# Making the second LayerNorm, the row table and the router's logits inside the attention units of a one-core transformer block

## What is computed

```python
mod = (silu(c) @ wmod).reshape(8, 6, 1, -1)          # sa, ca, ga, sb, cb, gb for each batch
ga, gb = sign(ga) * max(|ga|, 0.25), the same for gb
h = layernorm(x) * (1 + ca) + sa
x = x + ga * attention(h)                            # 16 heads of 16, rope, causal, Wo and bias
h = layernorm(x) * (1 + cb) + sb                     # the second LayerNorm
logits = h @ switch_w + switch_b                     # router over 8 experts, top 1
y = gelu(h @ w1[e] + b1[e]) @ w2[e] + b2[e]          # e = argmax of a token's logits, F = 1024
x = x + gb * (y * max softmax(logits))
```

## Time and profile before

| | before |
|---|---|
| median of 3 runs | 946.27 us |
| the three runs | 940.78, 946.27, 946.91 us |
| the profiled execution's own time | 946.43 us |
| its span, first to last instruction | 944.7 us |
| PE, DVE, ACT, POOL busy | 82%, 70%, 51%, 32% of the span |
| PE's mean granted clock | 0.899 of full |

### The profile page before, as it was taken

One profiled execution on the slowest core, in us unless ns is written; L12 is line 12 of the kernel. 1 busy time (PEld: TensorE's weight loads), 2 busy tenths in 40 slices (PEclk: granted clock), 3 DMA queues, 4 the chain that ended last, 5 costly groups with the idle time before them and its releaser, 6 DMA issues. The chain is left out here.

```text
span 944.7 us, 20373 instructions
## 1 busy us (share of the span) xinstructions
PE 771.2 (82%) x7362; PEld 469.0 (50%) x7362; DVE 659.4 (70%) x1270; ACT 481.4 (51%) x886; POOL 298.7 (32%) x377
## 2 busy tenths in 40 slices
PE   5859999999999999999887737730189999999994
PEld 3423444444444444444433327730177777777773
DVE  4857888788887888878764158879436666666664
ACT  1426666666666666666666115468144444444442
POOL 4303333232232323323222024357303333333331
PEclk9969999999999999999998656555579999999998
DMA  6153000010200102001010067767202222222200
GB/s 203 35 132 81 24 2 1 21 48 1 68 1 17 53 1 68 2 11 35 2 46 1 22 204 244 229 172 230 83 12 82 88 85 84 61 72 78 81 23 1
DMA packets 48523, 63.88 MB, mean 68 GB/s; under 512 B 9028, under 2 KB 42925, under 8 KB 48304
## 3 DMA queue, kind: packets, MB, share of 16 engines
q1 hardware_dynamic: 43440, 45.80, 16.1%
q0 software_dynamic: 4992, 16.81, 5.9%
HBM read 52.71 MB, written 17.73 MB: 75 GB/s over the span
## 5 line engine op out<-in xcount | busy, mean ns | idle before, releaser
L792 DVE TENSOR_REDUCE row_max<-ps_max 128x2 f32<-128x1024 f32 (+2 forms) x192 | 200.0, 1042 | 58.5 <-PE ps_max L461 55.8
L653 ACT ACTIVATE prob<-ps_sc 128x1024 f32<-128x1024 f32 (+1 forms) x192 | 169.3, 882 | 116.0 <-PE ps_sc L488 113.5
L314 POOL TENSOR_SCALAR_AFFINE_SELECT prob<-prob 128x512 f32<-128x512 f32 x128 | 84.0, 656 | 308.6 <-ACT prob L653 308.4
L1428 PE MATMUL ps_h<-tok_t,w_hi 128*128 128x128 f16 x1248 | 140.3, 222 | 2.5 <-issue 1.7
L1428 PEld LDWEIGHTS ps_h<-tok_t,w_hi 128*128 x1248 | 109.9, 99 | 44.2 <-issue 5.7
L1428 PE MATMUL ps_h<-tok_t,w_lo 128*128 128x128 f16 x624 | 122.8, 222 | 0.0
L1444 PE MATMUL ps_y<-w_both,hid_hi 128*128 x312 | 119.6, 384 | 0.8 <-DVE hid_lo L1503 0.8
L1482 ACT ACTIVATE hid<-ps_h,b_t 128x128 f32<-128x128 f32 x312 | 89.0, 372 | 45.3 <-PE ps_h L1428 45.2
L1501 DVE CAST hid_hi<-hid 128x512 f16<-128x512 f32 x78 | 36.7, 470 | 99.4 <-ACT hid L1482 99.3
L501 PE MATMUL ps_pv<-prob,v_sb 128*32 128x512 f32 (+3 forms) x1024 | 97.0, 452 | 0.0
L102 POOL DMA_INDIRECT slots<-row_dram,token x39 | 42.5, 1090 | 165.0 <-DVE y L1517 151.2
(11 more groups left out here) (224 smaller groups left out, 1417.0 us busy)
## 6 DMA issues: line engine op xcount, KB each, us to landing
raw<-w SPq DMA_DIRECT2D x32, 512.0 KB, 5.1
xs<-x SPq DMA_DIRECT2D x8, 512.0 KB, 4.6
xr<-x SPq DMA_DIRECT2D x8, 512.0 KB, 3.6
row_dram<-gates_dram SPq DMA_DIRECT2D x1, 4096.0 KB
row_dram<-xr SPq DMA_DIRECT2D x8, 512.0 KB, 3.5
x<-row_dram SPq DMA_DIRECT2D x8, 512.0 KB, 5.0
row_dram<-rows SPq DMA_DIRECT2D x8, 512.0 KB, 4.4
prob<-wmod SPq DMA_DIRECT2D x1, 1536.0 KB, 8.5
```

Source lines behind the costliest of these rows:

```text
L314: nc.gpsimd.affine_select(out=diag, in_=diag, compare_op=ALU.is_ge, fill=0.0, base=0, pattern=[[0, HG], [1, P]], channel_multiplier=-1).th ...
L653: nc.scalar.activation(p_kb[:, :, first * L:(first + n) * L], ps_sc[:, :, 0:n * L], ACT.Exp, scale=SCALE).then_inc(exp_done, 1)
L792: nc.vector.tensor_reduce(dst, ps_max[:, :, 0:n * L].rearrange("p j (m l) -> p j m l", m=n), AX.X, ALU.max).then_inc(max_done, 1)
L1428: last = mm(o, w[:, :, k, f, :][:, bass.ds(e, 1), :].rearrange("p e m -> p (e m)"), tok_t[:, j % 2, part, k, :], start=(n == 0 and f % HF ...
```

## The change

The work of the second LayerNorm, of the h rows and of the logits leaves `route_part` and goes into the units and the tail of `attention_part`.

- **Rows.** `xr` becomes `rows`, with h in columns 0 to 255 and x1 in 256 to 511, float32, stored as one piece for a batch. After `residual`, DVE does `row_statistics` in shot 2. POOL does `modulate_row` at the end of the unit: a power, one subtract and multiply, one multiply by a row of 1+cb and one add of a row of sb, all 128x256 float32. The rows of ga, 1+cb and sb come by `load_mods`, two batches held at a time. PE no longer makes the transposed form of these modulations.
- **Logits.** Seven units (`LAG`) behind, PE transposes h in shot 0 (`h_transposes`, two float32 transposes), ACT copies (`keep_h`), and once for each batch PE makes eight products and one transpose, with ACT copies.
- **Tail.** Each of the last batch's four tiles has a bank of its own (`tail_banks`). The rows, transposes and logits of the last tiles follow there.
- **`route_part`** holds only routing, b1, b2 and the weight halves: 6 buffers in place of 4, the first four chunks loaded during the last units, no loops. POOL makes the low halves of chunks 0 to 17, DVE those of 18 to 31, after the routing chain. SP stores the probabilities after the load of chunk 24, which waits for DVE's low half of chunk 18. POOL fetches after its 18 chunks.
- **`expert_part`.** The table holds h as float32, so PE makes two float32 transposes for four float16 ones, ACT copies the high half (128x256) and DVE makes the low half (`low_tokens`, 128x256), ahead of `halves(j)`.

```diff
+LAG = 7
+N_RAW = 6
+N_EARLY = 4
+POOL_CHUNKS = 18
...
             for b in range(2, B):
...
+                store_rows(b - 2)
+                load_mods(b)
                 load_xr(b)
+            for n in range(N_EARLY):
+                load_chunk(sp, n)
...
+            def modulate_row(Y):
+                pool.wait_ge(row_var, Y + 1)
+                nc.gpsimd.tensor_tensor(row_rstd[:, at:at + 1], row_eps[:, at:at + 1], neg_half[:, :], ALU.pow).then_inc(row_rs, 1)
...
+                nc.gpsimd.tensor_scalar(h, rows[:, par, t, D:2 * D], row_mv[:, at, 0:1], row_rstd[:, at:at + 1],
+                                        ALU.subtract, ALU.mult).then_inc(row_hat, 1)
+                nc.gpsimd.tensor_tensor(h, h, mod_rows[:, par, 1, :], ALU.mult).then_inc(scaled_done, 1)
+                nc.gpsimd.tensor_tensor(h, h, mod_rows[:, par, 2, :], ALU.add).then_inc(h_done, 1)
...
                 clear_future(U, 3)
+                if U >= QT + 1:
+                    modulate_row(U - QT - 1)
+            for Y in range(NT - QT - 1, NT):
+                modulate_row(Y)
...
+                    if s == 0 and Z >= 0:
+                        pe.wait_ge(gated_done, X)
+                        h_transposes(Z, ps_nd)
+                    if s == 1 and Z >= 0:
+                        pe.wait_ge(htr_kept, Z + 1)
+                        if Z % QT == QT - 1:
+                            logit_products(Z // QT, ps_nd)
+                        if Z % QT == 0 and Z:
+                            logit_transposes(Z // QT - 1, ps_nd)
...
             for X in range(NT - QT, NT):
-                att_transposes(X, NU)
-                project_out(X)
+                att_transposes(X, tail_banks[X % QT])
...
+                project_out(X, tail_banks[X % QT])
...
+            def row_statistics(Y):
+                dve.wait_ge(x1_done, Y + 1)
+                nc.vector.bn_stats(row_bn[:, :], rows[:, par, t, D:2 * D]).then_inc(row_stats, 1)
+                dve.wait_ge(row_stats, Y + 1)
+                nc.vector.bn_aggr(row_mv[:, at, :], row_bn[:, :]).then_inc(row_mv_done, 1)
+                dve.wait_ge(row_mv_done, Y + 1)
+                nc.vector.tensor_scalar(row_eps[:, at:at + 1], row_mv[:, at, 1:2], LN_EPS, None, ALU.add).then_inc(row_var, 1)
...
                     if s == 2 and T + 1 < NT:
                         statistics(T + 1)
+                    if s == 2 and X > 0:
+                        row_statistics(X - 1)
...
+            for n in range(N_RAW, CHUNKS):
+                sp.wait_ge(lo_of[n % N_RAW], turn(n) - 1)
+                load_chunk(sp, n)
+                if n == POOL_CHUNKS + N_RAW:
+                    sp.wait_ge(gate_done, 1)
+                    sp.dma_start(row_dram[:, AT_P:AT_P + 1].rearrange("(t p) o -> p (t o)", p=P), gate_p,
...
+            for n in range(POOL_CHUNKS):
+                pool.wait_ge(scaled_of[n % N_RAW], scaled_turn(n))
+                nc.gpsimd.tensor_tensor(half_of(w1_lo, w2_lo, n), raw_of(n), half_of(w1_hi, w2_hi, n),
+                                        ALU.subtract).then_inc(lo_of[n % N_RAW], 1)
...
-            batches(dve, step)
...
+            for n in range(POOL_CHUNKS, CHUNKS):
+                low_half(n)
...
+            low_tokens(0)
             for j in range(NJ):
+                if j + 1 < NJ:
+                    low_tokens(j + 1)
                 halves(j)
```

More of the change, by code:

```diff
@@ L380, in raw_gates @@
             def raw_gates(ps):
-                for n, part in enumerate((2, 5)):
+                for n, part in enumerate((5, 2)):
                     for k in range(KC):
@@ L386, in raw_gates, with raw_mods @@
                 last.then_inc(gates_ps, 1)
+            def raw_mods(ps):
+                for n, part in enumerate((4, 3)):
+                    for k in range(KC):
+                        last = mm(ps[0:B, n * D:(n + 1) * D], c_t[:, k, :], wmod_sb[:, k, part * D:(part + 1) * D],
+                                  start=(n == 0 and k == 0), stop=(k == KC - 1), skip_group_check=True)
+                last.then_inc(mods_ps, 1)
             pe.wait_ge(silu_done, 1)
@@ L1183, in _, with high_half @@
-            batches(act, step)
+            def high_half(n):
+                at = n % N_RAW
+                act.wait_ge(raw_loaded[at], 16 * turn(n))
+                nc.scalar.activation(half_of(w1_hi, w2_hi, n), raw_of(n), ACT.Copy, scale=W_SCALE).then_inc(hi_of[at], 1)
+                if n < POOL_CHUNKS:
+                    act.wait_ge(hi_of[at], turn(n))
+                    nc.scalar.activation(raw_of(n), raw_of(n), ACT.Copy, scale=W_SCALE).then_inc(scaled_of[at], 1)
+            high_half(0)
@@ L1192, in _ @@
+            for n in range(1, CHUNKS):
+                high_half(n)
         @block.vector
         def _(dve):
[L1194 to L1205 removed]
@@ L1221, in step @@
-            def step(i, u):
-                b = 2 * i + u
-                dve.wait_ge(rs, b + 1)
-                for t in range(QT):
-                    nc.vector.tensor_scalar(xhat[:, t, :], x1[:, u, t, :], mean_var[:, t, 0:1], rstd[:, t:t + 1],
-                                            ALU.subtract, ALU.mult).then_inc(xh, 1)
-                if not (last(i) and u):
-                    statistics(b + 1, 1 - u, 16 * (i + (u + 1) // 2 + 1))
-                if not isinstance(b, int) or b:
-                    e, half = before(i, u)
-                    low_half(e, 2 * half)
-                    low_rows(b - 1, 1 - u)
-                dve.wait_ge(xt_ps, b + 1)
-                for k in range(KC):
-                    nc.vector.tensor_scalar(h_t[:, u, k, :], ps_xt[k][:, :],
-                                            mod_t[:, 4 * KC + k, bass.ds(b, 1)], mod_t[:, 3 * KC + k, bass.ds(b, 1)],
-                                            ALU.mult, ALU.add).then_inc(ht_done, 1)
@@ L1410, in transposes @@
                 pe.wait_ge(slot_loaded[j % NB], loads_before(j))
-                ge(pe, x_kept, j)
-                for n in range(2 * KC):
-                    last = nc.tensor.transpose(ps_x[:, :].bitcast(F16)[:, n * P:(n + 1) * P],
-                                               slots[:, j % NB, 0:D].bitcast(F16)[:, n * P:(n + 1) * P], ident16[:, :])
+                ge(pe, x_lo_done, j)
+                for k in range(KC):
+                    last = nc.tensor.transpose(ps_x[:, k * P:(k + 1) * P], slots[:, j % NB, k * P:(k + 1) * P], ident[:, :])
                 last.then_inc(x_ps, 1)
```

552 lines of the change are left out of this document (256 added, 296 removed).

## The result

The changed kernel takes 915.4 us (median of 4 runs, 912.6 to 916.2) against 944.5 us for the kernel before (4 runs beside it, 940.8 to 946.9): ratio 0.970, with a 95% interval of 0.967 to 0.973. The profiled execution has a span of 913.6 us for 944.7 before, 31.1 us less. 925.3 was forecast for it. So the sign and the range held, and the forecast was 11.7 us too cautious. The working has to be read term by term, because its misses have both signs and partly cancel: that the total came this close is in part luck.

A forecast was written before the change was run, and what follows sets the result against it. PE and DVE in turn were taken to bound the units, and a serial chain and weight loads the gap. 944.7 + 27 + 2.4 - 52.8 + 4 = 925.3 us of span, 927 us time; range 908 to 946.

The forecast's parts named there:

- What bounds the units: Attention units: path runs over DVE in shots 1 to 4, over PE from shot 5 to the next shot 1.
- costs its full length: Units: work added on either engine's own stretch adds fully; statistics 0.81 us, h transposes 0.28 us; all units +27 us.
- my case: Whole kernel: the forecast's main outcome, 927 us, own range 916 to 938 us, chance 0.50.
- the first rival: Units pay 10 us, not 27, PE being about as late as DVE in shots 2 and 3; 910 us, chance 0.20.
- The tail: Last copy of u to route part: separate banks save, added rows and logits cost; 26.4 us for 24.0, +2.4.
- The chain: Routing chain: 25.9 us without POOL's hold-ups, plus 19 operations lengthened by 1.8 us, 60 us; bounds 48 and 65.
- Behind the chain: Chain's end to PE's first expert work: b2 operations, low halves, chunk turns, SP transfers 20 us, plus 1.7 to PE's start.
- The gap as a sum: Route part to PE's expert start: 0.3 + 60 + 20 + 1.7 = 82 us for 134.8, -52.8.
- the gap is set by the weights, not the chain: Gap rival: 32 chunks at 3.1 us each take 99 us, +17 on 82; 944 us, chance 0.06.
- The experts: Expert tiles: two float32 transposes cost PE more than four float16 ones, +2.3 to 5.5 us, taken as +4.
- the slower outcome: Units: PE's clock falls as its busy share drops to some 90%; +46 us, 973 us, chance 0.08.
- POOL's row operations blocked nothing on DVE in the units: Units, rival judged here: POOL's row operations block DVE about 0.6 us a unit, +17 us; 944 us, chance 0.16.

The follow-up runs named there:

- two edits: Changed kernel with row statistics moved to shot 0, ratio 0.968; changed kernel with the probabilities' store behind chunk 12 and b2 transfers behind all chunks, ratio 0.969.
- a third: Changed kernel with six slot buffers and the last four rows' 128x256 operations on DVE, held against six buffers alone (0.957): ratio 0.954.

## Why the prediction was right, and where it was not

Forecast minus measured, the spans differ by 11.7 us: units 8.5 too dear, tail 0.7 too cheap, gap 5.4 too cheap, experts 9.2 too dear. The sum came out near because two misses went against the other two.

**What bounds the units** was read rightly. Work put on DVE between shot 1 and the maxima of shot 3 showed as PE's wait of 0.70 us. Work put on PE in shot 0 cost 0.22. But "costs its full length" was too much: 1.09 us a unit was forecast and 0.68 measured. The statistics cost 0.56 and not 0.81. They moved the maxima by 0.73, and PE gave 0.12 of its wait back in shot 5, where it had stood a little for ACT's exponentials: its scores there began 0.23 us behind the max scores' last products before, and 0.11 after. That makes 0.78 us in three units of four. In the fourth this wait for the exponentials was longer,

```profile
298.77 0.29 PE L488 MATMUL ps_sc<-q_t,k_t 64*128 64x128 f16 x4 [0.33 <-ACT prob L653]
```

and such a unit took 15.09 us and not 14.70. The longer unit absorbs this whole, so the fourth unit costs only 0.39 more, and the mean is 0.68. I had added the two costs to a mean that held these idle times. The logit products, 1 us in the forecast, cost nothing: all units from the eighth on take 15.48. The lead (up to the seventh copy) and the last units cost 2.5 and 2.4 us, for 1.6 and 3.0 in the forecast. Of the 2.5, 1.4 lie ahead of the first copy of u, which comes anywhere from 85.7 to 88.0 us in executions of kernels that are alike up to there. The sum is +18.5 and not +27, within the bounds of 10 and 40 and halfway between my case and the first rival's 10. That rival's reason was that PE is about as late as DVE in shots 2 and 3. In the kernel before it was so, to within 0.1 us (PE's products ahead of shot 4 start at 310.27 and take 1.07), but this saved only 0.03 of the 0.73 us.

**The tail**: +3.1 for +2.4, and this closeness is luck. The forecast took PE at half clock throughout, and the profiled execution had 0.77 of full. In three other profiles of the same tail code, with 0.50 from 550 to 560 us, the tail took 28.7, 28.7 and 29.1 us, so +4.7 to +5.1. The forecast's own terms don't give its 26.4 us either: 24.0 - 4.8 + 1.9 + 0.8 + 2.9 + 4 is 28.8, or 24.7 without the 4.1 us that lie behind the last residual before. The banks gave 4.1 us for nearly 5. POOL's four operations took 3.2 us a row and not 2.9. The subtract and multiply with two scalars for each partition is the slow one, 1.22 us, the others are 0.72:

```profile
562.36 1.22 POOL L382 TENSOR_SCALAR rows<-rows,row_mv,row_rstd 128x256 f32<-128x256 f32 x1
563.67 0.72 POOL L385 TENSOR_TENSOR rows<-rows,mod_rows 128x256 f32<-128x256 f32 x1
```

What I missed is that in the tail they have no cover: four rows in a row on POOL, with the last row done 3.45 us behind the one before it.

**The chain**: 57.4 us for 60, with 17 lengthened operations of about 2 us where some 19 were expected. The step behind it, 12 operations by 1.8 us in the kernel before and a chain of 25.9 us without them, was tried directly: 27.0 us.

**Behind the chain** the step failed in size: 30.0 us for 21.7. I had put 2 us for SP's four other transfers between chunks 24 and 25, and they took 4.9. I had put 5.1 us of landing and 7.4 us for one turn. The rows of ACT in the changed kernel show chunk 25, issued at 635.09, in use at 641.39, and the last two chunks at 652.40 and 653.79:

```profile
641.39 1.06 ACT L1214 ACTIVATE w_hi<-early 128x1024 f16<-128x1024 f32 x1 [7.10 <-DMA early<-w]
...
652.40 1.06 ACT L1214 ACTIVATE w_both<-early 128x1024 f16<-128x1024 f32 x1 [2.36 <-DMA early<-w]
653.79 1.06 ACT L1214 ACTIVATE w_both<-early 128x1024 f16<-128x1024 f32 x1 [0.33 <-DMA early<-w]
```

Of the last two, chunk 30 was issued at 639.73 and chunk 31 when chunk 25's low half was done, at 643.7:

```profile
639.73 4.38 SPq L100 DMA_DIRECT2D early<-w  x2
```

From issue to use they needed 12.7 and 10.1 us, for 5.1 in the forecast. The four gathers were under way beside them, and the DMA engines were 82% busy; that this is the reason is likely and was not tried. The landing time of 5.1 us, a median over the kernel before, did not hold where eight loads, a store and four gathers are issued within some 16 us.

**The gap as a sum** hid what the total could not show: chain and rest are no separate terms. How many chunks POOL makes sets both, the one down and the other up, and the run with 12 chunks says by how much: 10.5 us off the chain are worth 2.2. The rival "the gap is set by the weights, not the chain", to which I gave 0.06 and 99 us, was right for the stretch behind the chain and wrong in size, since the gap is 87.4. It was not right as it stood, for the stream of chunks stands still while the chain ends (the 13.87 us above).

**The experts** went the other way, -5.2 us for +4. The two float32 transposes take PE exactly what the four float16 ones took in the earlier trace rows, 0.39 us, with the next product 0.22 behind:

```profile
877.81 0.39 PE L1405 MATMUL ps_x<-ident,slots 128*128 128x128 f32 x2
878.03 0.38 PE L1436 MATMUL ps_y<-w_both,hid_hi 128*128 x1
```

So the term that I put at +2.3 to +4 is nothing, and the tile's period is 5.82 us in both kernels. Nor was 0.28 us, read at L403, the price of two float32 transposes in the units, where doubling them cost 0.22. 5.7 us came from the smaller excess over that period (12.0 for 17.7), most of it from rows that were less late, and 0.5 were lost at the ends. I had not looked at PE's waits for gathered rows at all. The kernel before had 7.2 us of them by name. Why the changed kernel has fewer was not tried; on another chip it had 15.9.

**The other rivals.** Full clock in all of 100 to 480 us, at 92% busy: the slower outcome did not come. POOL's row operations blocked nothing on DVE in the units. One collision moved, that of DVE with POOL's mask: before it lengthened `xhat` (0.72 us for 0.41) in most units, after it `k_aug` (0.85 for 0.42). DVE's copy of q_t, the next operation that PE's work sets, starts 0.65 us behind PE's transposes for it and started 0.64 behind them before, so this does not show in the unit's length.

## What to carry to other kernels

Work taken out of a serial stretch and put into a full one pays by the difference. Price it where it lands, on the engine that ends the wait there, and take off what idle time the longer period swallows. Where a queue of loads is held by consumers that stand behind a serial chain, count the loads that are still to come when the chain ends, and not the chain alone: shortening it by moving their work behind it was nearly an even trade here. And measure a small gain beside the kernel that it starts from, on the same chip and at the same clock level: two edits seemed to bring nothing, and a third too, until each was held against a kernel under its own conditions.

## What was not expected of the hardware

- The same program has 2.5 us of waits for gathered rows on one chip and 15.9 us on another, and its ratio to the kernel before moves from 0.970 to 0.978. With two more buffers no such wait is left on any of the three chips.
- Three stores of 4 KB each (the bias parts) held SP's queue for 4.36 us, as long as it takes a weight chunk of 512 KB to land (a median of 4.4). They do so only right behind the store of 4096 single elements; elsewhere they take 1.8 us.
- Two float32 transposes of 128x128 take PE 0.39 us, as four float16 ones do.
- In the tail the granted clock of one and the same stretch is 0.98 in one execution of the changed kernel and 0.50 in another. The same tail takes 24.5 us in one execution (0.82 in that stretch) and 27.3 in another (0.50), with the four rows on DVE.
